# Masks of key tiles copied into PSUM by ScalarE, other bank counts for rows and key tiles, and products at the end of a fused attention, expert and filter kernel

## The reference

```
x = x + attention(x)        # 16 heads of 16, boolean mask, softmax, Wo, RMS norm, scale and shift by cond
x = x + experts(x)          # 8 experts of three layers (256-512-512-256), the best 2 per token
x = x + low_rank(x)         # 256 -> 64 -> 64 -> 256, scaled by the conditioning
x = x + quaternions(x)      # rotation of 64 quaternions per token, with a gate
```

```
scores = einsum('bhsd,bhtd->bhst', q, k) * D ** -0.5
scores = where(mask, -inf, scores)
attn   = softmax(scores, axis=-1)
out    = einsum('bhst,bhtd->bhsd', attn, v)
```

## Time and profile before

| what | us |
|---|---|
| median of three runs | 1181.97 (1180.37 to 1187.44) |
| span of the profiled execution, first to last instruction | 1176.1 |
| median less that span | 5.9 |
| TensorE busy | 1132.8 |
| VectorE busy | 814.5 |
| ScalarE busy | 734.6 |
| GpSimd busy | 524.7 |
| attention, first to last copy of maxima rows | 569.8 |

### The profile page before, as it was taken

How to read it: one execution, slowest core, us unless ns; L and a number is a source line. 1 busy time by engine, 2 the same in 40 slices (tenths; PEclk the granted TensorE clock), 3 DMA queues, 4 the chain that set the end, 5 groups by cost and what they waited for, 6 DMA issues and landing times.

```text
span 1176.1 us, 23436 instructions
## 1 busy us (share of the span) xinstructions
PE 1132.8 (96%) x7525; PEld 770.1 (65%) x7582; DVE 814.5 (69%) x2327; ACT 734.6 (62%) x1628; POOL 524.7 (45%) x837
## 2 busy tenths in 40 slices
PE   8899999999999999998988999999999999999988
PEld 4333433434334343342426999999999999999968
DVE  5888888787897878978774444346555555677747
ACT  2466667666676766666566656756666565666645
POOL 8324145583764846747471565346223222222220
PEclk8999999999999999999999999999999999999999
DMA  8655637468275572662726596936665765723536
GB/s 219 205 179 185 211 108 227 132 199 247 86 232 187 171 233 87 219 207 97 279 102 223 160 309 217 360 72 175 175 189 157 224 209 153 248 47 67 164 90 215
DMA packets 101616, 213.65 MB, mean 182 GB/s; under 512 B 10917, under 2 KB 71341, under 8 KB 93046
## 3 DMA queue, kind: packets, MB, share of 16 engines
q1 hardware_dynamic: 86038, 192.42, 49.8%
q0 software_dynamic: 14304, 18.69, 8.7%
q10 hardware_dynamic: 1152, 1.05, 0.4%
HBM read 239.28 MB, written 74.29 MB: 267 GB/s over the span
## 4 chain that ended last, share of the span: by engine, by line
PE 43%; POOL 2%; DMA 2%; DVE 2%; issue 1%; ACT 1%; SPq 1%; POOLq 0%; ACTq 0%
PE bank L1080 37%; PE bank L1239 1%; PE bank L1095 1%; DMA x<-yout,rows 1%; PE bank L1109 1%; PE bank L1199 1%; POOL routed L1952 1%; PE bank L1181 1%; DMA routed<-xw,idx 1%; PE bank L1274 0%; PE bank L1219 0%; POOL run L840 0%; DMA w_parts<-in_W 0%; POOL gt L840 0%; DVE tb L840 0%
## 5 line engine op out<-in xcount | busy, mean ns | idle before, releaser
L1615 DVE CUSTOM_DVE_ANT_0 junk<-bank,mneg 128x512 bf16<-128x512 f32 x512 | 335.6, 683 | 92.1 <-PE bank L1151 91.3
L1347 ACT ACTIVATE pt<-bank 128x512 f32<-128x512 f32 x512 | 301.8, 595 | 150.1 <-PE bank L1166 102.7
L1962 POOL DMA_INDIRECT x<-yout,rows x78 | 123.2, 1579 | 287.3 <-ACT yout L1425 242.7
L1080 PE MATMUL bank<-hid,w 128*128 128x256 f32 x1872 | 243.5, 287 | 3.8 <-DVE hid L1763 3.8
L1080 PEld LDWEIGHTS bank<-hid,w 128*128 128x128 f32 x1872 | 230.1, 191 | 5.7 <-issue 4.3
L1763 DVE TENSOR_TENSOR hid<-full,hid 128x256 fp32r<-128x256 f32 x312 | 132.3, 427 | 142.3 <-ACT full L1420 140.9
L1415 ACT ACTIVATE hid<-bank,biases 128x256 fp32r<-128x256 f32 x312 | 149.3, 479 | 96.1 <-PE bank L1080 94.7
L1166 PE MATMUL bank<-mneg,identb 128*128 128x512 bf16 x391 | 148.7, 380 | 0.0
L1420 ACT ACTIVATE full<-bank,biases 128x256 f32<-128x256 f32 x312 | 148.4, 476 | 0.0
L1080 PE MATMUL bank<-rowsT,w 128*128 128x256 f32 x936 | 123.0, 285 | 1.2 <-issue 1.2
L1181 PE MATMUL bank<-pt,vaug 128*17 128x512 f32 x1024 | 123.2, 599 | 0.7
(11 more groups left out here) (183 smaller groups left out, 1463.8 us busy)
## 6 DMA issues: line engine op xcount, KB each, us to landing
w<-split_weights SPq DMA_DIRECT2D x80, 1024.0 KB
w<-split_weights SPq DMA_DIRECT2D x40, 2048.0 KB
split_weights<-w_parts SPq DMA_DIRECT2D x64, 512.0 KB, 3.8
w_parts<-in_W SPq DMA_DIRECT2D x64, 256.0 KB, 4.5
split_parts<-parts SPq DMA_DIRECT2D x28, 384.0 KB, 2.6
rows<-routed SPq DMA_DIRECT2D x39, 258.0 KB, 3.6
stacks<-split_parts SPq DMA_DIRECT2D x36, 256.0 KB, 5.2
qst<-split_parts SPq DMA_DIRECT2D x24, 256.0 KB, 5.0
```

The costliest lines, as they stand in the source:

```text
L1080: product = T.matmul(ps, w[p], x[q], start=(k == 0 and n == 0), stop=(k == len(weights) - 1 and n == 2))
L1347: A.activation(pt[n % len(pt)][:, :], bank[3 + n % 2][:, :], ACT.Exp, scale=float(D) ** -0.5).then_inc(exped.sem, 1)
L1615: V.tensor_tensor_reduce(junk[n % 2][:, :], bank[n % 3][:, :], mneg[:, 0, st, :], 1.0, FLOOR, ALU.add, ALU.max, rowmax[gi % 2][:, hh, st:s ...
L1962: G.indirect_dma_start(x2_dram, bass.IndirectOffsetOnAxis(ap=rows[j % NS][:, tt, E + 1:E + 2].bitcast(U32), axis=0), yout[j % NY][:, tt], ...
```

## The change

Rows get two banks (0, 1), key tiles three (3, 4, 2). For all groups but the first, the heads with hh = 1 and hh = 3 of each key tile row are "seeded", eight of a group's 16 tiles: ScalarE copies `mneg` of that tile row into the bank, and TensorE's column product adds to it (start off), without the mask product. ScalarE writes the copy for the tile three places ahead right behind the exponential that frees its bank, and waits for that exponential. `trial_products` runs at the end of TensorE's program, after the last sum; nothing reads what it writes.

```diff
+ROW_BANKS = 0, 1
+COL_BANKS = 3, 4, 2
+SEEDED_HEADS = (1, 3), (1, 3), (1, 3), (1, 3)
+    seeded = signal("seeded", [(gi, kt, hh) for gi, kt, hh in cols_at if gi and hh in SEEDED_HEADS[kt]])
+        def trial_products():
+            plain = ident[:, :].bitcast(BF16)
+            lower, higher = slice(0, P // 2), slice(P // 2, P)
+            lanes = [x2T_hi[0][n * P // 2:n * P // 2 + 48, 0] for n in range(2)]
+            wide = [plain[part, :].unsqueeze(1).to_broadcast([P // 2, 2, E]) for part in (lower, higher)]
+            def score(ps, half, n, stop):
+                T.matmul(ps[:, :], lanes[half][:, n % 4 * P:(n % 4 + 1) * P], lanes[half], start=True, stop=stop)
+            def half_mask(ps, half, stop):
+                T.matmul(ps[:, :], plain[half * P // 2:(half + 1) * P // 2, 0:P], wide[half], start=False, stop=stop)
+            def values():
+                for hh in range(GH):
+                    T.matmul(bank[5][32 * hh:32 * hh + D + 1, :], x2T[0][:, 0, 0:D + 1], x2T[0][:, 0], start=True, stop=True)
+            def square():
+                T.matmul(bank[4][:, 0:P], ident[:, :], ident[:, :], start=True, stop=True)
+            def pair(n):
+                score(bank[(7, 3)[n]], 0, n, True)
+                score(bank[(6, 2)[n]], 1, n, True)
+            pe.wait_ge(*summed.at((B - 1, ST - 1)))
+            for n in range(8):
+                here, there = n % 2, 1 - n % 2
+                if n:
+                    half_mask(bank[4 + there], there, True)
+                score(bank[4 + here], here, n, False)
+                half_mask(bank[4 + here], here, False)
+                score(bank[6 + here], there, n, True)
+            half_mask(bank[4 + here], here, True)
...
+            for n in range(2):
+                for half in range(2):
+                    lane = x2T[0][half * P // 2:(half + 1) * P // 2, 0]
+                    T.matmul(bank[7 - half][:, :], lane[:, n * P:(n + 1) * P], lane, start=True, stop=True)
...
+            for n in range(4):
+                half = n // 2
+                T.matmul(bank[half][half * P // 2:(half + 1) * P // 2, :], plain[half * P // 2:(half + 1) * P // 2, 0:P // 2],
+                         wide[half], start=True, stop=True)
...
-                if n >= 3:
-                    pe.wait_ge(*max_found.at(rows_at[n - 3]))
+                if n >= len(ROW_BANKS):
+                    pe.wait_ge(*max_found.at(rows_at[n - len(ROW_BANKS)]))
...
-                pe.wait_ge(*(exped.at(cols_at[n - 2]) if n >= 2 else v_ready.at((0, ST - 1))))
+                seed = (gi, kt, hh) in seeded.value
+                if seed:
+                    pe.wait_ge(*seeded.at((gi, kt, hh)))
+                else:
+                    pe.wait_ge(*(exped.at(cols_at[n - len(COL_BANKS)]) if n >= len(COL_BANKS) else v_ready.at((0, ST - 1))))
...
-                limit = (gi, kt, hh) in cleared.value
+                limit = seed or (gi, kt, hh) in cleared.value
...
-                                   start=True, stop=limit)
+                                   start=not seed, stop=limit, skip_group_check=seed)
...
+        trial_products()
...
+                after = n + len(COL_BANKS) - 0
+                if after < len(cols_at) and cols_at[after] in seeded.value:
+                    act.wait_ge(masks_made, MASKS)
+                    act.wait_ge(*exped.at(cols_at[after - len(COL_BANKS)]))
+                    A.activation(col_bank(after)[:, :], mneg[:, 1, cols_at[after][1], :], ACT.Copy).then_inc(seeded.sem, 1)
```

More of the change, by code:

```diff
@@ L768, in misc_bank, with row_bank, col_bank @@
         return bank[6 + n % 2], n >= 2 and evicted(misc_users[n - 2])
+    def row_bank(n):
+        return bank[ROW_BANKS[n % len(ROW_BANKS)]]
+    def col_bank(n):
+        return bank[COL_BANKS[n % len(COL_BANKS)]]
     def value_bank(b, st):
@@ L1111, in side_stage @@
                 product.then_inc(side_pe.sem, 1)
+        def trial_products():
[24 more added lines that the diff above has]
+            half_mask(bank[4 + here], here, True)
+            pair(0)
+            pair(1)
+            values()
+            pair(0)
+            pair(1)
+            square()
+            pair(0)
+            pair(1)
+            square()
+            values()
+            square()
+            pair(0)
+            pair(1)
+            values()
+            square()
+            pair(0)
+            pair(1)
+            for n in range(2):
+                for half in range(2):
+                    lane = x2T[0][half * P // 2:(half + 1) * P // 2, 0]
+                    T.matmul(bank[7 - half][:, :], lane[:, n * P:(n + 1) * P], lane, start=True, stop=True)
+            pair(0)
+            pair(1)
+            values()
+            for n in range(4):
+                half = n // 2
+                T.matmul(bank[half][half * P // 2:(half + 1) * P // 2, :], plain[half * P // 2:(half + 1) * P // 2, 0:P // 2],
+                         wide[half], start=True, stop=True)
@@ L1147, in tensor_program @@
                 n = row_place[gi, hh, st]
-                if n >= 3:
-                    pe.wait_ge(*max_found.at(rows_at[n - 3]))
+                if n >= len(ROW_BANKS):
+                    pe.wait_ge(*max_found.at(rows_at[n - len(ROW_BANKS)]))
                 stacks_loaded(pe, b, h // (H // 2))
-                T.matmul(bank[n % 3][:, :], qst[b % 2][0:KQ, h, st * P:(st + 1) * P], kst[b % 2][0:KQ, h, :],
+                T.matmul(row_bank(n)[:, :], qst[b % 2][0:KQ, h, st * P:(st + 1) * P], kst[b % 2][0:KQ, h, :],
                          start=True, stop=True).then_inc(row_scored.sem, 1)
@@ L1156, in tensor_program @@
                 n = col_place[gi, kt, hh]
-                ps = bank[3 + n % 2]
-                pe.wait_ge(*(exped.at(cols_at[n - 2]) if n >= 2 else v_ready.at((0, ST - 1))))
+                ps = col_bank(n)
+                seed = (gi, kt, hh) in seeded.value
[3 more added lines that the diff above has]
+                    pe.wait_ge(*(exped.at(cols_at[n - len(COL_BANKS)]) if n >= len(COL_BANKS) else v_ready.at((0, ST - 1))))
                 pe.wait_ge(dma_mrow[gi % 2], 16 * (gi // 2 + 1))
                 pe.wait_ge(constants_made, CONSTANTS)
-                limit = (gi, kt, hh) in cleared.value
+                limit = seed or (gi, kt, hh) in cleared.value
                 product = T.matmul(ps[:, :], kst[b % 2][0:KQ + SHIFTS, h, kt * P:(kt + 1) * P], qst[b % 2][0:KQ + SHIFTS, h, :],
-                                   start=True, stop=limit)
+                                   start=not seed, stop=limit, skip_group_check=seed)
                 if not limit:
@@ L1346, in scalar_program @@
                     act.wait_ge(*weighed.at(cols_at[n - len(pt)][:2]))
-                A.activation(pt[n % len(pt)][:, :], bank[3 + n % 2][:, :], ACT.Exp, scale=float(D) ** -0.5).then_inc(exped.sem, 1)
+                A.activation(pt[n % len(pt)][:, :], col_bank(n)[:, :], ACT.Exp, scale=float(D) ** -0.5).then_inc(exped.sem, 1)
+                after = n + len(COL_BANKS) - 0
[3 more added lines that the diff above has]
+                    A.activation(col_bank(after)[:, :], mneg[:, 1, cols_at[after][1], :], ACT.Copy).then_inc(seeded.sem, 1)
             elif name == "project_o":
@@ L1614, in vector_program @@
                     dve.wait_ge(*max_split.at((gi - 2,)))
-                V.tensor_tensor_reduce(junk[n % 2][:, :], bank[n % 3][:, :], mneg[:, 0, st, :], 1.0, FLOOR, ALU.add, ALU.max,
+                V.tensor_tensor_reduce(junk[n % 2][:, :], row_bank(n)[:, :], mneg[:, 0, st, :], 1.0, FLOOR, ALU.add, ALU.max,
                                        rowmax[gi % 2][:, hh, st:st + 1]).then_inc(max_found.sem, 1)
```

## The result

The changed kernel takes 1220.64 us (median of four, 1217.27 to 1222.88) where the kernel before takes 1181.33 beside it: ratio 1.0304, 95% interval 1.0262 to 1.0346. It is 39.3 us slower. The forecast was 1167, with a range from 1143 to 1196.

A forecast was written before the change was run, and what follows sets the result against it. TensorE was taken to set the pace in attention, with VectorE close behind in three of four groups. 1181.97 less 28 for attention plus 13 for the end gave 1167 us, range 1143 to 1196.

The forecast's parts named there:

- The end products: After the last sum: trial products run beside only 2.6 us of store, ending the span 13 us later (10 to 18).
- the 12.7 of full sharing: End of the kernel: lower bound in us for the trial products if halves of the array share as strips do.
- the 21.0 of one after another: End of the kernel: upper bound in us for the trial products if none share the array.
- The 3 us for changes between shapes: End of the kernel: estimated extra on top of 12.7 us of shared trial products, giving 15.7.
- ScalarE's price: Attention: dependent exponential and copy take 0.61 + 0.50 us; a group's eight copies cost 5.1 us of ScalarE.
- the two counts: ScalarE's time in a batch's four groups: upper 19.1, 17.2, 19.2, 15.4 us; lower, with overlap, 17.1, 15.3, 17.3, 13.5.
- The row banks: Attention: with two row banks VectorE may be two tiles behind, not three; TensorE can wait up to 0.61 us each time.
- 0.2 us a group: Attention: deduction for fresh waits of TensorE on the two row banks, 6 us in all; upper bound 0.9 a group.
- Rival three: Attention: two row banks tie TensorE to VectorE; with 15 stalls 2.2 us a batch slower, 1213 us in all; chance 0.14.
- What the mask products are worth: Attention: removing 248 mask products saves TensorE 54.1 us of work, 7.0 us a batch.
- Attention gains 28 us: Attention stage: 34 us gained over 31 groups, less 6 us for fresh row-bank waits; half of TensorE's lost work.
- 71.2 us a batch: Attention: four groups together instead of 75.6 us, from 19.4, 17.3, 19.0 and 15.5, with VectorE idle time in the last three.

## Why the prediction was wrong

- **The end products**: 13 us forecast, 13.2 alone, 13.0 in the trace. Right, and so was the reading that halves of the array run beside each other: TensorE's tail took 15.4 us (1199.9 to 1215.3), between the 12.7 of full sharing and the 21.0 of one after another. The 3 us for changes between shapes were an estimate, measured at 2.7.
- **ScalarE's price**: 0.62 + 0.54 for exponential and copy against 0.61 + 0.50; its busy time of 17.7, 16.1, 18.2 and 14.5 us in the four groups lies within the two counts. The price of an instruction was right. What the copies cost in time was not: the sum gave ScalarE no term of its own in any group, since its count lay near TensorE's, and put together with the new banks the copies cost 20 us.
- **The row banks**: the step that failed first. I took off "0.2 us a group" for fresh waits of TensorE, with a bound of 0.9. Alone, without any copy, the two banks cost 3.0 to 3.3 us a batch, 0.8 a group, and 17 to 23 us in all. The bound was right and the choice was wrong: I reasoned that bursts would cover the stalls. They cover most: in one batch of banks alone (278.9 to 358.0) only six waits of row products are listed, 3.4 us together. But the two longest, 0.80 and 1.31 us, lie behind a single instruction of VectorE each, of 1.01 and 1.33 us, longer than the 0.61 a stall that I had as the most. Rival three had this mechanism, its time of 1213 is the nearest to what was measured, and I gave it 0.14. That its 2.2 us a batch lies so near the measured 2.3 is in part luck: it was 9.2 for stalls less 7.0 for the mask products, where the runs show 3.1 for the banks and 0.8 for the copies less 1.3 for the mask products.
- **What the mask products are worth**: 248 went, as the group L1245 with 200 products instead of 448 shows. "Attention gains 28 us" rested on 71.2 us a batch, a sum of the largest engine in each group plus an idle time for VectorE that I set by feeling at somewhat over half of what it was. Measured with masks left out and neither copies nor bank change, the batch is 74.5: 1.3 of 7.0 (1.8 at full clock), not 4.4. This is the second failed step. An engine that is 99% busy seemed the only bound; it was one of three partners that hand tiles to each other over two or three banks, and a shorter slot turned into waits at once, for VectorE (L1151) and for ScalarE (L1162).
- **What I had not counted**: the last groups, where ScalarE already was the path, 5.5 to 6.9 us in one stretch by the traces; and TensorE's clock, which the change lowers (see the last section).
- The forecast of TensorE a little below 95% busy, VectorE above 88%, ScalarE above 90%: measured 91, 81 and 85%. That all three fell short of it fits waits on banks and not a full engine.

Together: 13.2 (end) + 17.3 (banks) + 8.6 (copies, less what the mask products gave) = 39.1 of 39.3 us, each term good to 2 to 4. The last term is 20 for the copies less 11.4 for the mask products. Added up in the other order, attention is -15.0 (masks left out), +20.9 (banks), +20 (copies), 26.0 us slower, where 28 faster was forecast.

No kernel tried keeps every tile masked and its maxima whole and beats the kernel before.

## What to carry to other kernels

When three engines pass tiles through a few banks, work taken from the busiest one can be worth much less than its own length: leave the work out in a trial before building its replacement (here it gave 15 us of 54). A bank moved from one queue to another must be priced by the longest of the consumer's other instructions in the dense stretches, not by averages over a group. And a step that moves work to an idler engine should be looked at in the stretch where that engine is the path, at the end of a stage, as well as in the steady pattern.

## What the runs showed of the hardware

In these traces TensorE is granted less clock where the change makes it wait. The windows of the batch from the 26th copy of maxima rows on, for the change without end products, for the whole change, whose attention program is the same, and for banks alone, have a granted clock of 0.91, 0.96 and 0.98 of full speed:

```profile
514.20:597.10 82.90, 72.42 (x366) 26.02 (x365) 61.75 (x180) 64.71 (x140) 40.20 (x85) 0.91 0.46 147
```
```profile
511.80:592.80 81.00, 68.98 (x363) 24.93 (x361) 62.37 (x181) 64.44 (x140) 40.38 (x86) 0.96 0.47 151
```
```profile
515.60:594.20 78.60, 71.91 (x396) 29.02 (x394) 61.75 (x180) 47.90 (x108) 40.00 (x86) 0.98 0.49 155
```

One stretch at 1.2 GHz in the change without end products, and the window before it, where TensorE is busy 6.19 of 8.20 us:

```profile
575.00:583.20 8.20, 6.19 (x34) 1.51 (x33) 7.30 (x20) 7.31 (x14) 6.73 (x9) 1.00 0.30 100
583.20:590.00 6.80, 6.75 (x24) 1.13 (x24) 4.87 (x12) 3.12 (x6) 2.60 (x4) 0.50 0.61 166
```
```profile
585.03 0.63 PE L1226 MATMUL bank<-kst,qst 96*128 96x512 bf16 x1
585.46 0.63 PE L1241 MATMUL bank<-qst,kst 98*128 98x512 bf16 x1
585.88 0.63 PE L1245 MATMUL bank<-mneg,identb 128*128 128x512 bf16 x1
586.45 3.62 PE L1260 MATMUL bank<-pt,vaug 128*17 128x512 f32 x16
```

Products start 0.43 us apart instead of 0.218, as at the lower of the clock's two levels (1.2 and 2.4 GHz), and a weighing takes 3.62 us instead of 1.91. What this costs can be read where the same program ran at two clocks. The batch above took 82.9 us at 0.91 and 81.0 at 0.96. With the masks left out on the old banks, three batches at full clock took 73.8 to 74.1 us, and the next, at 0.97, 76.2.

Over the whole profiled execution the granted clock is 0.994 before, 0.991 for banks alone, 0.986 for the whole change and 0.980 without its end products. That makes 14, 22, 34 and 48 us at the lower level. At most half of such time is lost, so for banks alone the clock can account for at most 4 us more than before, but for the change for up to 10 to 17 (an estimate from these clocks). The clock thus has a part in the times with copies, and in those with masks left out (0.986 and 0.984 on the old and the new banks), of a size that no run here settles; the row banks' cost stands without it, since their steady batches all ran at full clock.
